# The stack pieces' transfers walk their source with the head's sixteen rows outermost

## The reference

```
qkv = x @ Wqkv;  q, k, v per head
for i in range(16):                                  # heads, one after the other
    q_rot, k_rot = rotary(q[:, i]), rotary(k[:, i])
    att = einsum('btd,bsd->bts', q_rot, k_rot) * scale
    if cascade_bias is not None:
        att = att + cascade_w[i - 1] * cascade_bias  # from the head before
    att = softmax(where(causal, -inf, att))
    head_outputs.append(att @ v[:, i])
    cascade_bias = mean(att, axis=1, keepdims=True)
out = concatenate(head_outputs) @ Wproj
```

## Time and profile before

| what | value |
|---|---|
| median of three runs | 3525.03 us |
| the profiled execution's own time | 3523.01 us |
| its span in the profile | 3521.2 us |
| TensorE clock granted, mean | 0.965 |
| busy: PE, ACT, DVE, POOL | 89%, 88%, 74%, 61% of the span |
| DMA queue of SP (q1) | 240144 packets, 323.19 MB, 31.6% of 16 engines' time |
| DMA queue of POOL (q0) | 14976 packets, 37.34 MB, 3.7% |

### The profile page before, as it was taken

How to read it: one execution, slowest core, us unless ns; L and a number is a source line. 1 busy time by engine, 2 the same in 40 slices (tenths; PEclk the granted TensorE clock), 3 DMA queues, 4 the chain that set the end, 5 groups by cost and what they waited for, 6 DMA issues and landing times. The chain is left out here.

```text
span 3521.2 us, 93094 instructions
## 1 busy us (share of the span) xinstructions
PE 3140.9 (89%) x29688; PEld 1533.7 (44%) x29688; DVE 2615.6 (74%) x7854; ACT 3085.7 (88%) x8904; POOL 2138.6 (61%) x6194
## 2 busy tenths in 40 slices
PE   5799899998999889999999998998999998998955
PEld 3233333333444434444444443444444443444644
DVE  6566666666777687887888888887888887777754
ACT  2799999999988999998989999998998999888733
POOL 5566656655555467776666666776666655555345
PEclk8899999999999999999999999999999999999987
DMA  4322322323333323434434333444423332344364
GB/s 150 101 71 73 86 57 73 88 64 91 95 100 100 103 73 111 120 113 125 128 98 132 111 82 91 116 120 140 113 85 121 106 104 84 108 115 141 101 194 126
DMA packets 256700, 370.68 MB, mean 105 GB/s; under 512 B 47829, under 2 KB 163293, under 8 KB 256208
## 3 DMA queue, kind: packets, MB, share of 16 engines
q1 hardware_dynamic: 240144, 323.19, 31.6%
q0 software_dynamic: 14976, 37.34, 3.7%
q10 hardware_dynamic: 1088, 4.19, 0.4%
HBM read 259.76 MB, written 104.40 MB: 103 GB/s over the span
## 5 line engine op out<-in xcount | busy, mean ns | idle before, releaser
L1529 DVE CUSTOM_DVE_ANT_0 att_a<-scores,window 128x128 f32<-128x128 f32 (+7 forms) x2048 | 1489.9, 754 | 519.8 <-PE scores L1216 346.1
L1390 ACT ACTIVATE att_a<-att_a,neg_max 128x128 f32<-128x128 f32 (+7 forms) x2048 | 1595.6, 779 | 88.7 <-DVE neg_max L1529 81.3
L1402 ACT ACTIVATE att_t<-scores 128x1024 f32<-128x1024 f32 (+7 forms) x2048 | 1330.4, 650 | 130.7 <-PE scores L1234 109.1
L1232 PE MATMUL scores<-q_stack,k_stack 104*128 104x512 bf16 (+3 forms) x3072 | 824.9, 334 | 165.7 <-DVE neg_max L1529 65.8
L1250 PE MATMUL pv<-att_t,v_sb 128*32 128x256 f32 (+7 forms) x16384 | 919.8, 301 | 7.4 <-ACT att_t L1402 5.1
L1216 PE MATMUL scores<-k_stack,q_stack 99*128 99x512 bf16 (+3 forms) x3072 | 692.8, 333 | 72.5 <-ACT att_t L1402 36.6
L1250 PEld LDWEIGHTS pv<-att_t,v_sb 128*32 128x32 f32 x16384 | 328.9, 108 | 595.8 <-issue 549.0
L1232 PEld LDWEIGHTS scores<-q_stack,k_stack 104*128 104x128 bf16 x3072 | 257.7, 98 | 570.7 <-DVE neg_max L1529 222.1
L1234 PE MATMUL scores<-identb,mask 128*128 128x128 bf16 x2048 | 454.5, 222 | 0.0
L1855 POOL TENSOR_SCALAR biasv<-col_sum,w_cas 128x8 f32<-128x8 f32 x240 | 87.5, 365 | 566.4 <-ACT att_t L1402 561.9
L1402 ACT ACTIVATION_READ_ACCUMULATOR att_t<-scores 128x1 f32 x2048 | 426.1, 208 | 0.0
(11 more groups left out here) (360 smaller groups left out, 4351.4 us busy)
## 6 DMA issues: line engine op xcount, KB each, us to landing
runner_r<-in_experts SPq DMA_DIRECT2D x137, 384.0 KB
qk_parts<-of_proj SPq DMA_DIRECT2D x128, 384.0 KB
of_proj<-in_xt SPq DMA_DIRECT2D x28, 1024.0 KB
q_stack<-qk_parts SPq DMA_DIRECT2D x256, 96.0 KB
k_stack<-qk_parts SPq DMA_DIRECT2D x256, 96.0 KB
q_stack<-qk_parts SPq DMA_DIRECT2D x256, 64.0 KB
k_stack<-qk_parts SPq DMA_DIRECT2D x256, 64.0 KB
head_out<-o_sb SPq DMA_DIRECT2D x252, 64.0 KB
```

The costliest lines, as they stand in the source:

```text
L1232: engine.matmul(scores[:, c0:c1], ks[0:ROWS_B, j * P:(j + 1) * P], qs[0:ROWS_B, j * P + c0 - base:j * P + c1 - base], start=True, stop=True)
L1390: engine.activation(taken, taken, EXP, scale=-1.0, bias=neg_max[:, n, i:i + 1], accum_out=row_sum[:, n, i:i + 1]).then_inc(s_exp_a, 1)
L1402: engine.activation(att_t[:, ring:ring + end - base], scores[:, base:end], EXP, accum_out=col_sum[:, n, j:j + 1]).then_inc(s_exp_b, 1)
L1529: engine.tensor_tensor_reduce(out=att_a[:, ring:ring + end - base], in0=scores[:, base:end], in1=window[:, T - (end - base):T], op0=ALU.ad ...
```

## The change

Only the order in which the source of a piece is walked changes. Before, the source has the copies (three or two blocks) outside and the 16 rows of a head inside, [n, d, t]; now it has the 16 rows outside and the copies inside, [d, n, t]. The destination is the same run of 48, 32 or 16 partition rows, filled in the source's order. So a row of the stack that held (block n, dim d) at place 16n + d now holds it at place 3d + n (or 2d + n). It is so for q and k alike, and a contraction doesn't mind the order of its rows. The 16-row piece has a count of one outside, and its transfer stays as it was. The number of transfers, their bytes, their rows of 2 KB, the waits and the order of the instructions on every engine are unchanged.

```
                 else:
                     part = qk_parts[0, piece:piece + 1, own, group * SLOTS + slot, :].broadcast_to([end - first, HD, T])
-                engine.dma_start(stack[first * HD:end * HD, h % 2, slot, :], part).then_inc(s_stack[h % 2][slot], 16)
+                engine.dma_start(stack[first * HD:end * HD, h % 2, slot, :],
+                                 part.rearrange("n d t -> d n t")).then_inc(s_stack[h % 2][slot], 16)
```

## The result

| | before | changed |
|---|---|---|
| median | 3522.02 us (4 runs, 3515.62 to 3527.89) | 3466.23 us (4 runs, 3460.03 to 3471.5) |
| ratio | 1 | 0.9841, 95% interval 0.9816 to 0.9867 |
| profiled execution | 3523.01 us | 3471.50 us |

The change takes 55.8 us away; 3480 was forecast, with 3450 to 3514 as the range. A second comparison gave 0.9818 (0.9791 to 0.9844).

A forecast was written before the change was run, and what follows sets the result against it. PE and ACT share the limit, both standing still when shift transfers wait behind full queues. 3523.0 - 39 (main stage) - 6 (first stage) = 3478, plus 2.0 for the median: 3480 us, range 3450 to 3514.

The forecast's parts named there:

- What bounds the kernel: Later main stage: PE and ACT share the limit; PE's form B matmul waits for the shift transfer 20 times, 38.8 us.
- the stop at 2657: Main stage: shift transfer issued at 2657.31, PE waits 3.73 us, ACT stands still 6.17 us; all 3.73 us should go.
- Who fills the few queues: DMA: 48-row pieces run on three engines, 32-row pieces on two; fullest queues take 5.6 us a set, 1.0 after.
- The main stage: Shift transfers land earlier: 33 us of PE time back, worth 39 us, between 15 and 64 us.
- The lower end of the range: Main stage: ACT or PE catches up half afterwards, so only 0.5 x 29 = 15 us is gained.
- The first stage: Tails of sends and loads on a few engines shorten: 6 us gained, bounds 0 and 10 us.
- four tails of 1 to 2 us: First stage: ends of bursts on a few engines, 6 us together; the burst itself stays.
- SP's issue: SP issuing a piece: 0.65 us before, 0.62 expected, so no change; ends 0.3 and 2.09 us.
- The slow rows: Rows in the new order may take 244 ns instead of 85, making a set's 12 rows 2.9 us, not 1.0.
- come back under another name: Rival, 9%: the next late thing, DVE's maxima or POOL's shift chain, decides; 0 to 10 us gained, 3515 to 3525.
- Both slower rivals: SP's issue at 1.7 us a piece, 3680 us, 2%; memory rows at 244 ns or worse, 3535 us, 2%.
- That the change does nothing: Rival, 3%: something else sets the engine count and pieces stay on few engines; 3525 us.

## Why the prediction was right

*What bounds the kernel.* The stops at form B's first matmul were the right place. Their disappearance (38.8 to 3.3 us), and the narrow transfers that bring them back in a kernel whose pieces are all wide, show it. In the stop at 2657 the records of packets show the queue itself: of the 64 packets of the shift and the bias transfer, 32 run by 2661, and the last 32 only between 2664.6 and 2665.8, after microseconds in which mostly rows of 2 KB run.

*Who fills the few queues.* The share of 0.19 read as three engines was right. The packet counts confirm both widths to the packet, and with them the Trainium skill's rule for the engine count ("DMA: Bandwidth & Descriptors", section "Why a DMA increments its semaphore by 16 and not by 1"): the largest number up to 16 that divides the outermost counts of both sides gives 3, 2 and 16 here. It gives five for the shift transfer, and the trace agrees: in the one of the earlier trace rows the forty packets of 256 bytes come with exactly five of 4 bytes. Which engines these are no run shows; that they are among those of the narrow transfers is shown by the lateness alone.

*The main stage.* 39 us was forecast and 44.4 came. I took 85% of PE's wait as coming back, 33 us; 35.5 us of it (91%) did. The factor from there to time was put at 39 / 33 = 1.2; it came out at 44.4 / 35.5 = 1.25. That the factor fits is in good part luck. The prediction argued it from both engines waiting at once, and its sum has no term for the clock, though the earlier trace rows have it at 0.98 in one stretch; the trace has 31.4 us less idling of PE and 13.0 us less for the same matmuls, and it is these 13 us that lift the factor above 1 (31.4 / 35.5 is 0.9). The lower end of the range, 0.5 x 29 = 15 us, uses a 29 that the prediction doesn't derive; half of its own 33 would be 16.5. ACT's wait for form B fell by 44.2 us, which is close to the stage's 44.4; one case doesn't show whether it is the better measure to start from.

*The first stage.* 6 us was forecast, 9.8 measured, at the edge of the bounds. I had counted four tails of 1 to 2 us. I had not followed that a send that lands late also holds up the chunk after it, the set of pieces and the x load behind. In the traces the slot's pieces are issued at 88.69 instead of 96.53 us, which is 7.8 us before the last tail is counted.

*SP's issue.* Forecast 0.62 us and no effect; it is 0.58 to 0.59 us, and the slack of 3.3 us a unit still covers it.

*The slow rows.* The reading of 244 ns a row from one microsecond was not borne out as a price: the share of the queue's packets is 31.7% for 31.6%, and in the records a packet of 2 KB on SP's queue takes 84 ns in the median in both orders, 113 ns in the mean before and 108 after. The Trainium skill's rule about power-of-two pitches ("DMA: Bandwidth & Descriptors", section "Latency and other measured facts") shows no effect here at 32 KiB. The prediction puts the rule too strongly: the Trainium skill has 207 GB/s at a pitch of 512 KiB, where the padded layout makes 214, and half of that only from 4 MiB on. No such pitch was run.

*The rivals.* The stops did not come back under another name: PE's wait for DVE's maxima at form B rose from 65.8 to 72.2 us, 6 us, against 35.5 us that went. The waits of ACT that the profile puts down to no engine rose too, from 11.3 to 19.3 us. Both slower rivals fell with the two points above. That the change does nothing is refuted by the packets.

Open are the tail's 2.7 us, for which one execution each is too little, the 93 us that the changed kernel's main stage still spends at the lower clock, and the 9 us by which the narrow transfer behind the shift rows costs more than its waits and its slower matmuls.

## What to carry to other kernels

In this kernel the outermost count of the source, 3, 2 or 16 against 48 or 32 rows of the destination, decided how many DMA engines carried a transfer, and the narrow ones held up later transfers behind them. Look for stretches in which an engine waits for a small transfer while the DMA share stands at a few sixteenths, and put a dimension of 16 rows outermost. What stands in a queue ahead of a transfer on the critical loop costs what exceeds the slack; the same transfer behind it cost a small part. And price a stop of PE by more than its length: read the granted clock behind it, and compare PE's busy time for the same count of matmuls.

## What the runs showed of the hardware

- Each DMA engine that takes part in a transfer issued by SP leaves one small packet of its own in the counts (13824, 6656 and 7168 more, as computed from the widths; five of 4 bytes with one shift transfer), so the page's packet count tells how wide transfers run.
- After a stop of PE of 3.7 us the granted clock fell from 1.00 to 0.50 about a microsecond into the work that followed, and was back at 1.00 three to four microseconds later. With 244 stops for shift rows the mean clock of the profiled execution was 0.904, with 2 of them (on another chip) 0.968.
- 50 MB more in the packets (421.1 instead of 370.7 MB on the pages) left the time at 0.9818 of before when it went over all engines.
- The median issue of a piece, over the three kinds, is 0.58 to 0.59 us where all run on 16 engines, and 0.64 to 0.65 us where two kinds run on two and three.
- A transfer of 32 rows on each of two engines ahead of a 10 KB transfer in each of 256 units made the kernel 17% slower; one of 8 rows cost 0.4%.
